# A mixture-of-experts stage: tokens become the stationary operand, expert weights are read in place

## The chip, the cores and the metric

The kernel runs on one core of one Trainium2 chip. The metric is the device time of one execution in microseconds. The times come from repeated executions; the profile is one execution recorded by the hardware profiler.

## What is computed

8192 tokens of width 256 are normalised (layer norm) to `xn`. A state-space block with a gated feed-forward works on `xn`, and so does a mixture of 32 experts with 8 chosen per token and one shared expert. The result is `x` plus both. The part that matters here, for the normalised tokens `h`:

```python
combine = (jax.nn.one_hot(tki, E, dtype=tkw.dtype) * tkw[..., None]).sum(1)
g = jax.nn.silu(jnp.einsum('th,eih->tei', h, w_gate))
u = jnp.einsum('th,eih->tei', h, w_up)
routed = jnp.einsum('tei,ehi->th', g * u * combine[:, :, None], w_down)
```

An expert has a hidden width of 128: gate and up weights are 128 x 256 each, the down weight 256 x 128. All is fp32.

## The kernel before

The program is written by hand engine by engine, with semaphores; the order of each engine's instructions is the order in the code. It has four parts. First, all tokens are normalised and routed. Then nine groups of 512 tokens go through the state-space block and feed-forward (`pe_group` and its like), while GpSimd scatters the token rows, sorted by expert, into `sorted_rows` in HBM, a row for each of the 8 choices. Then comes the expert stage. Last come the other seven groups, beside which GpSimd gathers the experts' results and VectorE sums them.

The expert stage treats 576 tiles of 128 sorted rows, each of one expert, in 288 pairs (`ALL`), 144 for each half of the tokens. All expert weights lie in SBUF in `big` (`WEXP` = 768 columns an expert: gate and up, then down). Which expert a tile has is known only at run time: `te_row` holds offsets, loaded into registers, four for two pairs. For pair n:

- SyncE loads two tiles of rows (`load_rows`, L427) into `rows[n % 4]`, a ring of 4. A row has 256 values and 32 routing weights.
- PE turns them: 4 transposes (`r_transpose`, L1255). ScalarE copies them out of PSUM to `rT` (L647).
- VectorE copies the gate/up weights of the pair's two experts from `big` to `wgu` (`copy_weights`, L1031), two pairs ahead.
- PE forms gate and up (`e_gu`, L1266), with weights stationary and tokens moving: 8 products, each 2 passes (a weight load and a matmul each) in the trace. The result has hidden units on the partitions.
- ScalarE takes the SiLU of gate (`e_gate`, L652), VectorE multiplies with up to `eh` (`e_hidden`, L1039).
- PE multiplies by the down weights (`e_down`, L1280), `eh` stationary and the weights moving in place out of `big`: 2 products of 256 columns, 4 passes.
- ScalarE and VectorE scale one tile each by the routing weight (`e_out`, L662 and L1048) to `ey`.
- SyncE stores the results (L449), and then loads the rows of pair n + 4.

PE's order in iteration n is `e_gu(n)`, `r_transpose(n+1)`, `e_down(n-1)`. ScalarE's is gate(n), `rT` copy(n+1), output(n-1). VectorE's is weight copies(n+2), hidden(n), output(n-1), and from pair 150 on a step of summing gathered results (L957, L964). SyncE's order is output store, rows load, and now and then a load of `parts` and a store of `out`. GpSimd scatters the second half's rows during the first part of the stage (until 853 us), and gathers the first half's results from 1042 us on.

Of the kernel before, what the change touches and what calls it, by code (L numbers as in the profile page):

```python
# [5 lines left out]
P = 128  # L6
# [3 lines left out]
ALU = mybir.AluOpType  # L10
# [39 lines left out]
def build(nc, x, log_lambda, BT, CT, D_skip, ssm_w, ssm_w_col, ffn_w_col, w13T, w2T, gateT, gate_bias, wexp,  # L50
# [29 lines left out]
    with ExitStack() as ctx:  # L80
# [3 lines left out]
        def sem(name):  # L84
            return ctx.enter_context(nc.semaphore(name))
# [91 lines left out]
        def take(n):  # L177
            at[0] += n
            assert at[0] <= ARENA
            return arena[:, at[0] - n:at[0]]  # L180
# [23 lines left out]
        wgu = [take(4 * INNER * 2).rearrange("p (s w) -> p s w", s=2) for _ in range(2)]  # L204
# [68 lines left out]
        wgu_ready = sem("wgu_ready")  # L273
# [58 lines left out]
        def scattered_all(eng, half):  # L332

            for j in range(4):
                eng.wait_ge(scattered[half][j], 16 * K * QUARTER)
# [3 lines left out]
        def _(sp):  # L339
# [106 lines left out]
            for n in range(ALL):  # L446
                sp.wait_ge(ey_act, n + 1)
                sp.wait_ge(ey_dve, n + 1)
                sp.dma_start(pair_rows(results, n), ey[n % RING]).then_inc(ey_stored[n % RING], 16)  # L449
                if n + RING == PAIRS:  # L450
                    scattered_all(sp, 1)
                if n + RING < ALL:
                    load_rows(n + RING)
                for i in summed_after(n + 6):
                    load_part(i)
                for i in summed_after(n - 2):
                    store_out(i)
            assert not summed_after(ALL - 2) and not summed_after(ALL - 1)

            sp.wait_ge(wgu_ready, ALL)  # L460
# [70 lines left out]
        def _(act):  # L531
# [107 lines left out]
            regs = [[act.alloc_register(f"act_expert{j}_{k}") for k in range(4)] for j in range(3)]  # L639

            def load_experts(n):
                act.load(regs[n // 2 % 3], te_row[0:1, HALVES * NTILE + 2 * n:HALVES * NTILE + 2 * n + 4])

# [12 lines left out]
            def e_out(n):  # L656

                e = act.snap(regs[n // 2 % 3][2 * (n % 2)], min_val=0, max_val=E - 1)
                act.wait_ge(ey_ready, n + 1)
                if n >= RING:  # L660
                    act.wait_ge(ey_stored[n % RING], 16 * (n // RING))
                nc.scalar.activation(ey[n % RING][:, 0, :], ps[:, 4 + 2 * (n % 2), 0:D], ACT.Copy,  # L662
                                     scale=rows[n % RING][:, 0, ds(e + D, 1)]).then_inc(ey_act, 1)
# [5 lines left out]
            for n in range(ALL):  # L669
                if n % 2 == 0:  # L670
                    load_experts(n)
                e_gate(n)
                if n + 1 < ALL:
                    rT_copy(n + 1)
                if n >= 1:
                    e_out(n - 1)
# [12 lines left out]
        def _(dve):  # L689
# [328 lines left out]
            offsets = [[dve.alloc_register(f"dve_offset{j}_{k}") for k in range(4)] for j in range(3)]  # L1018
            experts = [[dve.alloc_register(f"dve_expert{j}_{k}") for k in range(4)] for j in range(3)]

            def load_tables(n):
                dve.load(offsets[n // 2 % 3], te_row[0:1, 2 * n:2 * n + 4])
                dve.load(experts[n // 2 % 3], te_row[0:1, HALVES * NTILE + 2 * n:HALVES * NTILE + 2 * n + 4])

            def copy_weights(n):

                if n >= 2:
                    dve.wait_ge(egu_ready, n - 1)
                for s in range(2):
                    at_w = dve.snap(offsets[n // 2 % 3][2 * (n % 2) + s], min_val=0, max_val=(E - 1) * WEXP)  # L1030
                    last = nc.vector.tensor_copy(wgu[n % 2][:, s, :], big[:, ds(at_w, 4 * INNER)])  # L1031
                last.then_inc(wgu_ready, 1)

            def e_hidden(n):

                dve.wait_ge(eg_ready, n + 1)
                if n >= 2:
                    dve.wait_ge(ey_ready, n - 1)
                tt(eh[n % 2], eg[n % 2], ps[:, 2 + n % 2, :].rearrange("p (s u i) -> p s u i", s=2, u=2)[:, :, 1, :],  # L1039
                   ALU.mult).then_inc(eh_ready, 1)  # L1040

            def e_out(n):

                e = dve.snap(experts[n // 2 % 3][2 * (n % 2) + 1], min_val=0, max_val=E - 1)
                dve.wait_ge(ey_ready, n + 1)
                if n >= RING:
                    dve.wait_ge(ey_stored[n % RING], 16 * (n // RING))
                tsc(ey[n % RING][:, 1, :], ps[:, 5 + 2 * (n % 2), 0:D], rows[n % RING][:, 1, ds(e + D, 1)], None,  # L1048
                    ALU.mult).then_inc(ey_dve, 1)
# [5 lines left out]
            load_tables(0)  # L1055
            copy_weights(0)
            copy_weights(1)
            for n in range(ALL):
                if n + 2 < ALL:
                    if n % 2 == 0:  # L1060
                        load_tables(n + 2)
                    copy_weights(n + 2)
                e_hidden(n)
                if n >= 1:
                    e_out(n - 1)
                for i, j in sum_after(n):
                    sum_step(i, j)
            e_out(ALL - 1)
# [15 lines left out]
        def _(pe):  # L1084
# [173 lines left out]
            def e_gu(n):  # L1258

                pe.wait_ge(rT_ready, n + 1)  # L1260
                pe.wait_ge(wgu_ready, n + 1)
                for s in range(2):
                    for u in range(2):
                        for c in range(DC):
                            at_w = (2 * c + u) * INNER
                            last = mm(ps[:, 2 + n % 2, (2 * s + u) * P:(2 * s + u + 1) * P],  # L1266
                                      wgu[n % 2][:, s, at_w:at_w + INNER],
                                      rT[n % 2][:, (2 * s + c) * P:(2 * s + c + 1) * P],
                                      start=c == 0, stop=c == DC - 1)
                last.then_inc(egu_ready, 1)  # L1270

            def e_down(n):

                if n >= 2:
                    pe.wait_ge(ey_act, n - 1)
                    pe.wait_ge(ey_dve, n - 1)
                pe.wait_ge(eh_ready, n + 1)
                for s in range(2):
                    at_w = pe.snap(regs[n // 2 % 3][2 * (n % 2) + s], min_val=0, max_val=(E - 1) * WEXP)
                    last = mm(ps[:, 4 + 2 * (n % 2) + s, 0:D], eh[n % 2][:, s, :], big[:, ds(at_w + 2 * D, D)],  # L1280
                              start=True, stop=True)
                last.then_inc(ey_ready, 1)
# [6 lines left out]
            for n in range(ALL):  # L1289
                if n % 2 == 0:  # L1290
                    load_offsets(n)
                e_gu(n)
                if n + 1 < ALL:
                    r_transpose(n + 1)
                if n >= 1:
                    e_down(n - 1)
# [54 lines left out]
```

## Time and profile before

| | us |
|---|---|
| median of 3 runs | 1920.8 (1915.5 to 1921.8) |
| the profiled execution's own time | 1924.6 |
| its span, first to last instruction | 1922.9 |
| PE busy | 1772.2 (92%) |
| GpSimd busy | 1058.2 (55%) |
| VectorE busy | 1016.6 (53%) |
| ScalarE busy | 652.8 (34%) |
| mean granted TensorE clock | 0.968 |

PE is TensorE's matmul side and PEld its weight loads, which overlap it; DVE is VectorE, ACT ScalarE, POOL GpSimd, SP SyncE. A "q" behind an engine's name is its sequencer (register work, DMA issues). L1266 is line 1266 of the kernel. Matmul durations are modelled: starts can be trusted more than ends. The expert stage lies between 551 and 1552 us of the span.

### The profile page before, as it was taken

To read this page: it belongs to the slowest core of one execution; us is meant where nothing else is said; L and a number is where in the kernel's file an instruction comes from. 1 tells how busy PE (TensorE), PEld (TensorE's weight loads), DVE (VectorE), ACT (ScalarE), POOL (GpSimd) and SP (SyncE) were. 2 spreads that over 40 slices of the span, in tenths; PEclk is the share of its full clock that TensorE was granted. 3 is DMA by queue.
4 is the path that set the end of the run, shared out by engine and by line. 5 is a ranking of instruction groups with operands and counts; after the bars stand their busy time and mean duration, and the time that the engine had idled before them with its cause. 6 is when DMAs were issued, how large, how long until landed. Compare 5 with 4: busy or idle time off the path is not lost.

```text
span 1922.9 us, 30939 instructions
## 1 busy us (share of the span) xinstructions
PE 1772.2 (92%) x9896; PEld 1347.3 (70%) x9896; DVE 1016.6 (53%) x2464; ACT 652.8 (34%) x1349; POOL 1058.2 (55%) x1058
## 2 busy tenths in 40 slices
PE   6798898999989999999999999899989969999995
PEld 3454555666568888888988888788878846666663
DVE  6577456333334444444444656565656635565554
ACT  5621222222224444444444434343434422222220
POOL 0002777777777777750002655556555147777776
PEclk9898898999989999999999999999999979999997
DMA  6804334554668988985556888788777753333333
GB/s 208 257 22 138 136 127 162 198 213 157 237 225 276 286 272 282 284 261 175 175 171 199 255 242 250 242 243 245 237 238 241 212 168 113 114 114 101 107 103 105
DMA packets 262614, 374.53 MB, mean 195 GB/s; under 512 B 30917, under 2 KB 227641, under 8 KB 261689
## 3 DMA queue, kind: packets, MB, share of 16 engines
q1 hardware_dynamic: 212392, 227.51, 38.5%
q0 software_dynamic: 49920, 145.03, 22.9%
q8 instruction: 82, 1.34, 0.3%
q14 instruction: 76, 0.61, 0.1%
q10 hardware_dynamic: 144, 0.03, 0.0%
HBM read 189.47 MB, written 182.98 MB: 194 GB/s over the span
## 4 chain that ended last, share of the span: by engine, by line
PE 67%; DMA 17%; DVE 8%; issue 3%; SPq 2%; ACT 1%; DVEq 1%; POOL 1%; POOLq 0%; ACTq 0%
PE ps L1182 19%; DMA arena<-sorted_rows 16%; PE ps L1266 15%; PE ps L1199 11%; PE ps L1280 9%; PE ps L1255 6%; DVE arena L1048 2%; PE ps L1135 2%; PE ps L1164 1%; SPq L449 1%; PE ps L1151 1%; PE ps L1102 1%; PE ps L1174 1%; DMA big<-in_x 1%; POOL xe L524 1%
## 5 line engine op out<-in xcount | busy, mean ns | idle before, releaser
L524 POOL DMA_INDIRECT xe<-results,slots x512 | 537.4, 1050 | 524.7 <-DMA results<-arena 239.2
L1266 PE MATMUL ps<-arena 128*128 128x128 f32 x4608 | 590.5, 282 | 1.5 <-ACT arena L647 1.5
L1266 PEld LDWEIGHTS ps<-arena 128*128 128x128 f32 x4608 | 540.2, 193 | 66.0 <-ACT arena L647 65.9
L1031 DVE COPY arena<-big 128x512 f32 x576 | 226.6, 435 | 344.4 <-PE ps L1266 320.6
L513 POOL DMA_INDIRECT sorted_rows<-big,slots x256 | 257.6, 1006 | 85.0 <-issue 77.7
L1280 PE MATMUL ps<-big,arena 128*128 x1152 | 297.5, 381 | 0.3 <-DVE arena L1039 0.3
L513 POOL DMA_INDIRECT sorted_rows<-xe,slots x256 | 251.8, 983 | 78.0 <-issue 78.0
L1182 PE MATMUL ps<-arena,w 128*128 128x512 f32 x640 | 287.7, 592 | 0.0
L939 DVE TENSOR_TENSOR arena<-arena,ps 128x512 f32<-128x512 f32 (+1 forms) x128 | 88.1, 688 | 330.7 <-ACT arena L615 329.6
L615 ACT ACTIVATE arena<-ps 128x512 f32<-128x512 f32 (+1 forms) x128 | 76.3, 596 | 546.7 <-PE ps L1182 502.7
L652 ACT ACTIVATE arena<-ps 128x256 f32<-128x256 f32 x288 | 110.4, 383 | 378.8 <-PE ps L1266 378.8
L1255 PE MATMUL ps<-ident,arena 128*128 128x128 f32 x1152 | 180.7, 280 | 59.9 <-DMA arena<-sorted_rows 58.4
L1280 PEld LDWEIGHTS ps<-big,arena 128*128 128x128 f32 x1152 | 197.2, 191 | 15.4 <-issue 0.7
L647 ACT ACTIVATE arena<-ps 128x512 f32<-128x512 f32 x288 | 172.0, 597 | 102.7 <-PE ps L1255 91.9
L1182 PEld LDWEIGHTS ps<-arena,w 128*128 128x128 f32 x640 | 121.8, 190 | 118.8 <-issue 114.7
L1048 DVE TENSOR_SCALAR arena<-ps,arena 128x256 f32<-128x256 f32 x288 | 139.3, 484 | 122.2 <-PE ps L1280 120.8
L1199 PE MATMUL ps<-w,arena 128*128 128x256 f32 (+1 forms) x768 | 186.4, 386 | 1.8 <-DVE arena L939 1.8
L1255 PEld LDWEIGHTS ps<-ident,arena 128*128 128x128 f32 x1152 | 129.6, 142 | 79.4 <-DMA arena<-sorted_rows 71.3
L1199 PEld LDWEIGHTS ps<-w,arena 128*128 128x128 f32 (+1 forms) x768 | 143.1, 191 | 50.7 <-issue 31.2
L662 ACT ACTIVATE arena<-ps,arena 128x256 f32<-128x256 f32 x288 | 136.3, 473 | 109.1 <-PE ps L1280 109.1
L957 DVE TENSOR_TENSOR xe<-xe 128x1024 f32<-128x1024 f32 (+2 forms) x192 | 148.9, 775 | 9.8 <-DMA xe<-results,slots 7.2
L1182 PE MATMUL ps<-arena,shgu 128*128 128x512 f32 x256 | 123.5, 639 | 7.0 <-DVEq L793 7.0
(158 smaller groups left out, 1175.5 us busy)
## 6 DMA issues: line engine op xcount, KB each, us to landing
arena<-sorted_rows SPq DMA_DIRECT2D x288, 288.0 KB, 3.7
results<-arena SPq DMA_DIRECT2D x288, 256.0 KB, 2.8
big<-in_x SPq DMA_DIRECT2D x32, 512.0 KB, 4.3
sorted_rows<-big SPq DMA_DIRECT2D x2, 4608.0 KB, 16.9
xe<-results,slots POOLq DMA_INDIRECT x512, 3.3
out<-xe SPq DMA_DIRECT2D x64, 128.0 KB, 2.2
sorted_rows<-big SPq DMA_DIRECT2D x48, 144.0 KB, 1.8
big<-in_wexp SPq DMA_DIRECT2D x1, 5632.0 KB, 20.6
```

The lines of the kernel that those rows point to most:

```text
L513: pool.indirect_dma_start(out=sorted_rows[half], out_offset=bass.IndirectOffsetOnAxis(ap=slots[:, half * HT + t, k:k + 1], axis=0), in_=ro ...
L524: pool.indirect_dma_start(out=gathered_at[i % RING][:, k, :], out_offset=None, in_=results[half], in_offset=bass.IndirectOffsetOnAxis(ap=s ...
L647: nc.scalar.activation(rT[n % 2], ps[:, n % 2, :], ACT.Copy).then_inc(rT_ready, 1)
L662: nc.scalar.activation(ey[n % RING][:, 0, :], ps[:, 4 + 2 * (n % 2), 0:D], ACT.Copy, scale=rows[n % RING][:, 0, ds(e + D, 1)]).then_inc(ey ...
L957: do(tt(y[:, 0:m, :], y[:, 0:m, :], y[:, m:2 * m, :], ALU.add))
L1031: last = nc.vector.tensor_copy(wgu[n % 2][:, s, :], big[:, ds(at_w, 4 * INNER)])
L1048: tsc(ey[n % RING][:, 1, :], ps[:, 5 + 2 * (n % 2), 0:D], rows[n % RING][:, 1, ds(e + D, 1)], None, ALU.mult).then_inc(ey_dve, 1)
L1182: last = mm(ps[:, 2 + 2 * (s % 2) + u, :], w[:, u, c, lo:lo + P], src[:, c, :], start=c == 0, stop=c == DC - 1)
L1199: last = mm(ps[:, 6 + t // 2, (t % 2) * D:(t % 2 + 1) * D], h[c % HR][at_p, t * P:(t + 1) * P], w, start=False, stop=s == CH - 1 and t % 2 ...
L1255: last = tp(ps[:, n % 2, j * P:(j + 1) * P], rows[n % RING][:, s, c * P:(c + 1) * P], ident[:, :])
L1266: last = mm(ps[:, 2 + n % 2, (2 * s + u) * P:(2 * s + u + 1) * P], wgu[n % 2][:, s, at_w:at_w + INNER], rT[n % 2][:, (2 * s + c) * P:(2 * ...
L1280: last = mm(ps[:, 4 + 2 * (n % 2) + s, 0:D], eh[n % 2][:, s, :], big[:, ds(at_w + 2 * D, D)], start=True, stop=True)
```

## The change

The product's operands change sides. The turned tokens `rT` become the stationary operand of gate and up, and the weights move in place out of `big`, 256 columns (gate and up of one 128-row chunk) at once; VectorE's copies to `wgu` go. Now tokens lie on the partitions of the result, so the routing weight is applied in `e_hidden` as a per-partition factor, and not on the outputs. The hidden product must be turned before the down product: `h_transpose` (2 transposes) and VectorE's `ehT_copy` are new, and the down product and outputs come one iteration later. SyncE's loop issues `load_rows(m+4)` once `e_hidden(m)` is done, and the store of pair m - 2 behind it.

```diff
-        wgu = [take(4 * INNER * 2).rearrange("p (s w) -> p s w", s=2) for _ in range(2)]
+        ehT = [take(2 * P).rearrange("p (s n) -> p s n", n=P) for _ in range(2)]
...
-            for n in range(ALL):
+            for m in range(ALL + 2):
+                if m < ALL:
+                    sp.wait_ge(eh_ready, m + 1)
+                    if m + RING == PAIRS:
+                        scattered_all(sp, 1)
+                    if m + RING < ALL:
+                        load_rows(m + RING)
+                n = m - 2
+                if n < 0:
+                    continue
                 sp.wait_ge(ey_act, n + 1)
                 sp.wait_ge(ey_dve, n + 1)
                 sp.dma_start(pair_rows(results, n), ey[n % RING]).then_inc(ey_stored[n % RING], 16)
-                if n + RING == PAIRS:
-                    scattered_all(sp, 1)
-                if n + RING < ALL:
-                    load_rows(n + RING)
...
-            sp.wait_ge(wgu_ready, ALL)
...
-                nc.scalar.activation(ey[n % RING][:, 0, :], ps[:, 4 + 2 * (n % 2), 0:D], ACT.Copy,
-                                     scale=rows[n % RING][:, 0, ds(e + D, 1)]).then_inc(ey_act, 1)
+                nc.scalar.activation(ey[n % RING][:, 0, :], ps[:, 4 + 2 * (n % 2), 0:D], ACT.Copy
+                                     ).then_inc(ey_act, 1)
...
-                if n >= 1:
-                    e_out(n - 1)
+                if n >= 2:
+                    e_out(n - 2)
+            e_out(ALL - 2)
             e_out(ALL - 1)
...
             def e_hidden(n):
 
                 dve.wait_ge(eg_ready, n + 1)
                 if n >= 2:
+                    dve.wait_ge(hposed, n - 1)
+                for s in range(2):
+                    e = dve.snap(experts[n // 2 % 2][2 * (n % 2) + s], min_val=0, max_val=E - 1)
+                    last = nc.vector.scalar_tensor_tensor(eh[n % 2][:, s, :], eg[n % 2][:, s, :],
+                                                          rows[n % RING][:, s, ds(e + D, 1)],
+                                                          ps[:, 2 + n % 2, (2 * s + 1) * P:(2 * s + 2) * P],
+                                                          ALU.mult, ALU.mult)
+                last.then_inc(eh_ready, 1)
+
+            def ehT_copy(n):
+                dve.wait_ge(hposed, n + 1)
+                if n >= 2:
                     dve.wait_ge(ey_ready, n - 1)
-                tt(eh[n % 2], eg[n % 2], ps[:, 2 + n % 2, :].rearrange("p (s u i) -> p s u i", s=2, u=2)[:, :, 1, :],
-                   ALU.mult).then_inc(eh_ready, 1)
+                nc.vector.tensor_copy(ehT[n % 2], ps[:, 4 + 2 * (n % 2), D:2 * D].rearrange("p (s n) -> p s n", n=P)
+                                      ).then_inc(ehT_ready, 1)
...
-            load_tables(0)
-            copy_weights(0)
-            copy_weights(1)
             for n in range(ALL):
-                if n + 2 < ALL:
-                    if n % 2 == 0:
-                        load_tables(n + 2)
-                    copy_weights(n + 2)
+                if n % 2 == 0:
+                    load_experts(n)
                 e_hidden(n)
                 if n >= 1:
-                    e_out(n - 1)
+                    ehT_copy(n - 1)
+                if n >= 2:
+                    e_out(n - 2)
                 for i, j in sum_after(n):
                     sum_step(i, j)
...
                 pe.wait_ge(rT_ready, n + 1)
-                pe.wait_ge(wgu_ready, n + 1)
                 for s in range(2):
-                    for u in range(2):
-                        for c in range(DC):
-                            at_w = (2 * c + u) * INNER
-                            last = mm(ps[:, 2 + n % 2, (2 * s + u) * P:(2 * s + u + 1) * P],
-                                      wgu[n % 2][:, s, at_w:at_w + INNER],
-                                      rT[n % 2][:, (2 * s + c) * P:(2 * s + c + 1) * P],
-                                      start=c == 0, stop=c == DC - 1)
+                    at_w = pe.snap(regs[n // 2 % 3][2 * (n % 2) + s], min_val=0, max_val=(E - 1) * WEXP)
+                    for c in range(DC):
+                        last = mm(ps[:, 2 + n % 2, s * D:(s + 1) * D], rT[n % 2][:, (2 * s + c) * P:(2 * s + c + 1) * P],
+                                  big[:, ds(at_w + 2 * c * INNER, 2 * INNER)], start=c == 0, stop=c == DC - 1)
                 last.then_inc(egu_ready, 1)
 
-            def e_down(n):
-
+            def h_transpose(n):
                 if n >= 2:
                     pe.wait_ge(ey_act, n - 1)
                     pe.wait_ge(ey_dve, n - 1)
                 pe.wait_ge(eh_ready, n + 1)
                 for s in range(2):
+                    last = tp(ps[:, 4 + 2 * (n % 2), D + s * P:D + (s + 1) * P], eh[n % 2][:, s, :], ident[:, :])
+                last.then_inc(hposed, 1)
+
+            def e_down(n):
+                pe.wait_ge(ehT_ready, n + 1)
+                for s in range(2):
                     at_w = pe.snap(regs[n // 2 % 3][2 * (n % 2) + s], min_val=0, max_val=(E - 1) * WEXP)
-                    last = mm(ps[:, 4 + 2 * (n % 2) + s, 0:D], eh[n % 2][:, s, :], big[:, ds(at_w + 2 * D, D)],
+                    last = mm(ps[:, 4 + 2 * (n % 2) + s, 0:D], ehT[n % 2][:, s, :], big[:, ds(at_w + 2 * D, D)],
                               start=True, stop=True)
                 last.then_inc(ey_ready, 1)
...
                 if n >= 1:
-                    e_down(n - 1)
+                    h_transpose(n - 1)
+                if n >= 2:
+                    e_down(n - 2)
+            h_transpose(ALL - 1)
+            e_down(ALL - 2)
             e_down(ALL - 1)
```

## Rows read from the trace of the kernel before

**Rows 1.** The page, part 1: busy time and share of each engine.

```profile
PE 1772.2 (92%) x9896; PEld 1347.3 (70%) x9896; DVE 1016.6 (53%) x2464; ACT 652.8 (34%) x1349; POOL 1058.2 (55%) x1058
```

**Rows 2.** The page, part 4: the chain that ended last, by line.

```profile
PE ps L1182 19%; DMA arena<-sorted_rows 16%; PE ps L1266 15%; PE ps L1199 11%; PE ps L1280 9%; PE ps L1255 6%; DVE arena L1048 2%; PE ps L1135 2%; PE ps L1164 1%; SPq L449 1%; PE ps L1151 1%; PE ps L1102 1%; PE ps L1174 1%; DMA big<-in_x 1%; POOL xe L524 1%
```

**Rows 3.** Three stretches: length, busy PE, PEld, DVE, ACT, POOL, granted clock, DMA share, GB/s.

```profile
560.00:853.00 293.00, 280.76 (x2075) 251.79 (x2075) 139.17 (x345) 125.17 (x259) 223.82 (x228) 1.00 0.89 278
853.00:1040.00 187.00, 184.22 (x1389) 167.79 (x1388) 91.60 (x232) 84.18 (x174) 0.92 (x1) 1.00 0.59 175
1040.00:1550.00 510.00, 471.06 (x3416) 418.34 (x3415) 300.59 (x695) 206.82 (x427) 270.97 (x256) 0.99 0.79 239
```

**Rows 4.** Timeline, one pair at 903 us: start, duration, what, idle before it.

```profile
902.78 1.86 PEld L1266 LDWEIGHTS ps<-arena 128*128 128x128 f32 x16 [0.22 <-ACT arena L647]
...
903.09 0.47 ACT L662 ACTIVATE arena<-ps,arena 128x256 f32<-128x256 f32 x1 [0.37 <-PE ps L1280]
903.11 0.48 DVE L1048 TENSOR_SCALAR arena<-ps,arena 128x256 f32<-128x256 f32 x1 [0.22 <-PE ps L1280]
...
904.08 0.47 SPq L427 DMA_DIRECT2D arena<-sorted_rows  x1
...
904.66 0.60 PE L1255 MATMUL ps<-ident,arena 128*128 128x128 f32 x4
904.87 0.38 ACT L652 ACTIVATE arena<-ps 128x256 f32<-128x256 f32 x1 [1.30 <-PE ps L1266]
904.97 0.76 DVE L1031 COPY arena<-big 128x512 f32 x2 [1.38 <-PE ps L1266]
...
905.10 1.03 PE L1280 MATMUL ps<-big,arena 128*128 x4
905.30 0.60 ACT L647 ACTIVATE arena<-ps 128x512 f32<-128x512 f32 x1
905.65 0.41 DVE L1039 TENSOR_TENSOR arena<-arena,ps 128x256 f32<-128x256 f32 x1
905.95 1.86 PEld L1266 LDWEIGHTS ps<-arena 128*128 128x128 f32 x16 [0.22 <-ACT arena L647]
```

**Rows 5.** Line 1266: duration ns min/median/max, first and last start.

```profile
L1266 PEld LDWEIGHTS ps<-arena x4608: 186/192/338, 553.5 to 1548.8; 128*128 128x128 f32 x192
```

**Rows 6.** Waits of weight loads, 553 to 1552 us: total us, times, longest.

```profile
PEld ps L1255 <- DMA arena<-sorted_rows: 71.3, 92, 2.7
PEld ps L1266 <- ACT arena L647: 65.9, 287, 1.2
```

**Rows 7.** Row loads (L427): 880 to 960, then 1200 to 1350, then all.

```profile
DMA to landing us min/median/max: 2.9/3.0/4.4
...
L427 SPq DMA_DIRECT2D arena<-sorted_rows x42: 463/472/1057, 1199.6 to 1349.2; - x42
...
  PEld ps L1255: 19.7, 20
DMA to landing us min/median/max: 2.8/4.4/5.5
...
DMA to landing us min/median/max: 2.8/3.7/6.3
```

**Rows 8.** Timeline, the last pair of the stage.

```profile
1549.61 0.42 DVE L1039 TENSOR_TENSOR arena<-arena,ps 128x256 f32<-128x256 f32 x1 [1.68 <-ACT arena L652]
...
1550.28 0.73 PEld L1280 LDWEIGHTS ps<-big,arena 128*128 128x128 f32 x4 [0.66 <-issue]
```

**Rows 9.** Line 1247, the load of offsets on PE's sequencer: duration ns.

```profile
L1247 PEldq TENSOR_LOAD <-te_row x144: 328/522/894, 551.7 to 1542.4; - x144
```

**Rows 10.** Timeline, the first pair of the stage.

```profile
553.51 3.49 PEld L1266 LDWEIGHTS ps<-arena 128*128 128x128 f32 x16 [1.17 <-ACT arena L647]
```

**Rows 11.** A three-operand instruction (L908), and the longest summing step, 560 to 1552.

```profile
L908 DVE SCALAR_TENSOR_TENSOR arena<-big,rinv,skip_w x60: 459/479/544, 85.4 to 1841.8; 128x256 f32<-128x256 f32 x60
L957 DVE TENSOR_TENSOR xe<-xe 128x1024 f32<-128x1024 f32 x32 | 38.9, 1216 | 0.0
```

More of the change, by code:

```diff
@@ L272, in build @@
         rT_ready = sem("rT_ready")
-        wgu_ready = sem("wgu_ready")
+        hposed = sem("hposed")
+        ehT_ready = sem("ehT_ready")
         egu_ready = sem("egu_ready")
@@ L636, in _ @@
                 act_group(g, g + 1 < FIRST)
-            regs = [[act.alloc_register(f"act_expert{j}_{k}") for k in range(4)] for j in range(3)]
-            def load_experts(n):
-                act.load(regs[n // 2 % 3], te_row[0:1, HALVES * NTILE + 2 * n:HALVES * NTILE + 2 * n + 4])
             def rT_copy(n):
@@ L656, in e_out @@
             def e_out(n):
-                e = act.snap(regs[n // 2 % 3][2 * (n % 2)], min_val=0, max_val=E - 1)
                 act.wait_ge(ey_ready, n + 1)
@@ L669, in _ @@
             for n in range(ALL):
-                if n % 2 == 0:
-                    load_experts(n)
                 e_gate(n)
@@ L1015, in _, with load_experts @@
                 dve_group(g, g + 1 < FIRST)
[L1018 to L1032, printed above, removed]
+            experts = [[dve.alloc_register(f"dve_expert{j}_{k}") for k in range(4)] for j in range(2)]
+            def load_experts(n):
+                dve.load(experts[n // 2 % 2], te_row[0:1, HALVES * NTILE + 2 * n:HALVES * NTILE + 2 * n + 4])
             def e_hidden(n):
@@ L1037, in e_hidden @@
                 if n >= 2:
+                    dve.wait_ge(hposed, n - 1)
[9 more added lines that the diff above has]
+                if n >= 2:
                     dve.wait_ge(ey_ready, n - 1)
-                tt(eh[n % 2], eg[n % 2], ps[:, 2 + n % 2, :].rearrange("p (s u i) -> p s u i", s=2, u=2)[:, :, 1, :],
-                   ALU.mult).then_inc(eh_ready, 1)
+                nc.vector.tensor_copy(ehT[n % 2], ps[:, 4 + 2 * (n % 2), D:2 * D].rearrange("p (s n) -> p s n", n=P)
+                                      ).then_inc(ehT_ready, 1)
             def e_out(n):
-                e = dve.snap(experts[n // 2 % 3][2 * (n % 2) + 1], min_val=0, max_val=E - 1)
                 dve.wait_ge(ey_ready, n + 1)
@@ L1047, in e_out @@
                     dve.wait_ge(ey_stored[n % RING], 16 * (n // RING))
-                tsc(ey[n % RING][:, 1, :], ps[:, 5 + 2 * (n % 2), 0:D], rows[n % RING][:, 1, ds(e + D, 1)], None,
-                    ALU.mult).then_inc(ey_dve, 1)
+                nc.vector.tensor_copy(ey[n % RING][:, 1, :], ps[:, 5 + 2 * (n % 2), 0:D]).then_inc(ey_dve, 1)
             dve.wait_ge(te_loaded, 16 * 2 * HALVES)
@@ L1054, in _ @@
                 dve.wait_ge(part_stored[par], 16 * len(range(par, FIRST, 2)))
-            load_tables(0)
-            copy_weights(0)
-            copy_weights(1)
             for n in range(ALL):
-                if n + 2 < ALL:
-                    if n % 2 == 0:
-                        load_tables(n + 2)
-                    copy_weights(n + 2)
+                if n % 2 == 0:
+                    load_experts(n)
                 e_hidden(n)
                 if n >= 1:
-                    e_out(n - 1)
+                    ehT_copy(n - 1)
+                if n >= 2:
+                    e_out(n - 2)
                 for i, j in sum_after(n):
                     sum_step(i, j)
+            ehT_copy(ALL - 1)
+            e_out(ALL - 2)
             e_out(ALL - 1)
```

## The prediction

> **What bounds the kernel now.** Read the page from the top. TensorE (PE) is busy 92% of the span and no other engine above 55% [rows 1], but that is a share over the whole program, and the change touches one stage, the 288 expert pairs. The chain that ended last gives 16% of the span, about 307 us, to the load of a pair's rows [rows 2]. That figure must not be taken for idle time: the chain follows one ring of dependences (load, transpose, products, output, next load) and books the whole flight of each load, while PE works on other pairs under most of it. So I went to PE itself.
>
> Three stretches of the stage [rows 3], at 24 PE instructions a pair: 2075 instructions are 86.5 pairs in 293 us, 3.39 us a pair, while the second half is still scattered; 57.9 pairs in 187 us, 3.23 us, when GpSimd is nearly silent; 142.3 pairs in 510 us, 3.58 us, while results are gathered. The same work takes different times, and the stretch with the least foreign DMA traffic is the fastest.
>
> One pair of the quiet stretch [rows 4] shows the floor. The first weight load of `e_gu` starts at 902.78 and, one pair on, at 905.95: 3.17 us. Inside, 16 gate/up passes are (1.86 - 0.19)/15 = 0.111 us apart, 1.78 us; the 4 row transposes (0.60 - 0.27)/3 = 0.110 apart, 0.44; the 4 down passes (1.03 - 0.38)/3 = 0.217 apart, 0.87. That is 3.09. The missing 0.08 to 0.09 stands in the last row: the loads sat idle 0.22 us until ScalarE's copy `rT` (905.30 + 0.60 = 905.90) was done; the load wants to start some 0.1 before its matmul, and came 0.09 late.
>
> Over the stage, the first gate/up load starts at 553.5 and the last at 1548.8 [rows 5]; less 15 x 0.111, that is 993.6 us for 287 periods, where 287 x 3.18 = 912.7 would do. The excess is 81 us. The waits name it: the transpose's weight load waited 71.3 us in 92 places for the rows' DMA [rows 6] (each wait is counted from the end of a 0.19 us load, where the next could have started at 0.11, so 92 x 0.08 = 7 us more are hidden in it: 79). The other wait, 65.9 us in 287 places for the copy `rT`, is the 0.09 a pair above.
>
> Why are rows late? SyncE issues `load_rows(n+4)` after the output of pair n. In [rows 4] it goes out at 904.08 and its transpose comes at 904.66 + 3.17 = 907.83: 3.75 us of slack. Landing takes 3.0 us (median) in the quiet stretch, but 4.4 (up to 5.5) while gathers run, with 20 waits in 42 [rows 7]. The load is launched too late for its latency under load.
>
> **The change, part by part.**
>
> *PE, gate and up.* Eight products (16 passes of 128 columns) become four of 256 columns, 8 passes. Same shape and operands as the down product, which moves `big` over 256 columns at 0.217 a pass: 8 x 0.217 = 1.74 against 1.78, -0.04.
>
> *PE, hidden transposes.* Two more, same form as the row transposes: 2 x 0.110 = +0.22. Their wait (hidden of pair n-1) was satisfied most of a period before. The down product is now that of n-2 and waits for a copy also made in the period before.
>
> *PE, the copy's cover.* Between the row transposes and the next `e_gu` now lie 0.22 + 0.87 us in place of 0.87. Counted from the last row transpose (x = 904.66 + 0.33 = 904.99), `rT` is done at x + 0.91, and the first gate/up load would be due at x + 0.11 + 0.22 + 0.87 - 0.11 = x + 1.09. The wait now sits on a register operation (the offset into `big`), which before ran far ahead. From the end of a releaser to a plain load is 0.05 us (905.90 to 905.95) [rows 4]; over a register operation on ScalarE 0.13 (906.13 to 903.09 + 3.17 = 906.26) [rows 4]; on PE over two sequencer steps, at the stage's end, 0.25 (VectorE ends 1550.03, load at 1550.28) [rows 8]. The load thus starts at x + 0.96, 1.04 or 1.16: nothing, nothing, or 0.07 late. I take nothing, nearest to the single step: the old 0.09 goes. The table load (0.52, at most 0.89 us [rows 9]) now feeds the same iteration; it is queued before the wait, and there is room for it while PE is in the 1.5 us of transposes and down products.
>
> Sum of a period: 8 x 0.217 + 6 x 0.110 + 4 x 0.217 = 3.26 us against 3.17 to 3.18. **PE's own work becomes longer**, by 0.08 x 287 = 23 us over the stage.
>
> *SyncE, the order of loads.* `load_rows(m+4)` now waits for the hidden product of pair m, since the routing weight is applied there, and not for the outputs. With e_gu(m) starting at G: its last pass ends at G + 1.51 + 0.38 = G + 1.9, the gate takes 0.38 and starts 0.04 later, the two hidden instructions about 0.6, so the issue is near G + 3.1. The transpose comes at G + 3 x 3.26 + 1.74 = G + 11.5. Slack 8.4 us, against 3.75, and the longest landing of the whole stage is 6.3 [rows 7]. The store of a pair is issued one iteration later and a part load or output store may stand before a load; each holds the queue for about the 0.47 us of an issue [rows 4], covered by the slack. Behind the new wait stands the store of pair m-2, whose outputs come later still (near G + 3.9), so it loses nothing. The wait on the weight copies ahead of the late `x` loads goes as well, worth nothing: it was long satisfied. So the row waits go: -81 + 3 that I leave for stray ones and 2 for the first pair, which ran at half clock (its 16 loads took 3.49 us [rows 10]) and stays so. That is about -76.
>
> *VectorE.* Gone: two copies of 512 columns, 0.76 together, and the scaled output (0.48). In: two hidden products of 128 columns in place of one of 256 (0.41), a copy `ehT`, a plain output copy. Bounds for the two: 0.41 (same columns at once) to 2 x 0.48 (a three-operand instruction of twice the width [rows 11]); the copies 0.41 to 0.48 each. VectorE's pair is 1.2 to 1.9 us against 1.65, plus summing of at most 1.22 [rows 11] in a pair: under 3.26 either way. It costs the sum nothing; were its cover gone it would be the 0.2 us by which 3.1 nears 3.26. ScalarE only loses a register step.
>
> *Gathers.* GpSimd starts them when half 0 is stored, one iteration later: some 7 us after e_gu(145) starts, the eighth lands near +20, and the first sum is due near 5 x 3.26 + 3.9 = +20. A wait of 1 or 2 us, once, hidden by the hidden product's lead.
>
> *Tail.* After the last `e_gu`, a transpose (0.22, and 0.27 until its end), a copy (0.42), and the register step now stand before the last down product, and the hidden product is two instructions: +1.2 us. The late groups behind are unchanged and follow it one for one.
>
> **The sum.** New stage: 287 x 3.26 + 2 + 3 = 940.6; old 993.6; difference -53.0, with the tail -51.8. From the profiled execution's own time, 1924.6 (span 1922.9): 1873. The median of the runs is 3.8 lower: 1869, rounded **1870**. Its own range: no stray waits and a period of 3.25 give 1863; 10 us of stray waits and 0.03 a pair more, 1885.
>
> - *The row waits are throughput, not latency*, **slower than before** (8%). The 16 DMA engines are busy 0.89 and 0.79 in the stretches with waits, 0.59 without [rows 3]. If loads queue behind each other, launching them early only lengthens their landing; the point of decision is a landing over 8.4 us. Then the 81 us stay, and PE's extra 23 us hide under them or come on top: with the tail +1 to +24, so 1922 to 1945, and 1940 as its value, since most pairs have no wait to hide under. Against it: rows and results alone need 0.59 x 3.23 = 1.9 us of the engines a pair, so in the scatter stretch 0.89 - 1.9/3.39 = 0.33 is foreign, and 1.9/3.26 + 0.33 = 0.91 at the new pace: still below 1.
> - *VectorE turns into the wait* (4%): a gather that is late holds the queue of sums, hidden products and the new copy together. 0.1 us a pair in the 144 pairs with sums, and some row waits: 1885 to 1915.
> - *The clock falls* with the larger share of transposes (1%). The first pair, run at the lower level, shows the price: passes (3.49 - 0.23)/15 = 0.217 apart where later ones are 0.111 [rows 10], twice the time. A tenth of the stage's work at 1.2 GHz adds 94 us, 1964.
> - *The change does not do what it says*, that is passes over `big` at register addresses pace worse than 0.217 (2%): with 0.02 each, 8 x 0.02 x 287 = 46 us, 1916.
>
> **How the numbers follow.** Forecast 70%, the rivals 30%. 1853 to 1900 holds the forecast, what lies a little below it, and the exposed register step: 85% by these chances; the slower rivals stay outside. Within 0.3% (about 6 us, what a measurement of this kernel can tell) lie the last rival, the mild end of the throughput one and of the VectorE one, 4%. Slower are most of the throughput rival and the clock, 8%; faster 88%.
>
> **What would show it.** In the profile after: `e_gu`'s period 3.26 in the quiet stretch, with 8 passes 0.217 apart and no idle before them; almost no wait of the row transpose for DMA; SyncE's load issued about 8 us before its transpose; the stage from 553.5 to some 1500. A period of 3.3 or more with PE idle until ScalarE's copy is the first rival; landings of 8 us are the second. The prediction is wrong if either stands.

## The result: 1864 us, and where it came from

| kernel | median us | ratio to before, 95% interval |
|---|---|---|
| before | 1920.2 (1915.5 to 1921.8) | |
| changed | 1864.2 (1863.9 to 1868.5) | 0.9708 [0.9672, 0.9743] |

The change makes the kernel 3% faster; 1870 with a range of 1853 to 1900 was predicted. The profiled execution took 1864.3 us, with a span of 1862.4.

The page of the changed kernel, its busy times (part 1) and its chain by line (part 4), answering to [rows 1, 2]:

```profile
PE 1764.0 (95%) x8166; PEld 1323.1 (71%) x8168; DVE 949.2 (51%) x2464; ACT 627.5 (34%) x1349; POOL 1033.7 (56%) x1058
PE ps L1260 27%; PE ps L1178 19%; PE ps L1277 13%; PE ps L1195 11%; PE ps L1251 7%; PE ps L1270 3%; PE ps L1160 2%; PE ps L1131 2%; PE ps L1098 1%; PE ps L1147 1%; PE ps L1170 1%; DMA big<-in_x 1%; POOL xe L529 1%; PE ps L1091 1%; SPq L366 0%
```

In the new numbering L1251 is the row transposes, L1260 gate and up, L1270 the hidden transposes, L1277 the down products, L428 the row load. The row load had 16% of the chain [rows 2] and is gone from it. PE's busy time hardly moved (1772 to 1764 us); what went is the time between its instructions. The stage's stretches, read as [rows 3]:

```profile
560.00:853.00 293.00, 293.00 (x1626) 257.25 (x1625) 122.72 (x360) 122.91 (x270) 218.22 (x227) 1.00 0.89 287
853.00:1040.00 187.00, 187.00 (x1039) 164.17 (x1038) 78.30 (x231) 78.83 (x173) 6.70 (x7) 1.00 0.57 177
1040.00:1490.00 450.00, 449.14 (x2489) 394.00 (x2488) 264.68 (x683) 188.26 (x414) 244.43 (x249) 1.00 0.87 262
```

At 18 PE instructions a pair that is 3.24, 3.24 and 3.25 us a pair, where it was 3.39, 3.23 and 3.58. The quiet stretch became a little slower, the other two faster: foreign DMA traffic no longer shows in PE's pace. One pair on the timeline (start, duration, what), answering to [rows 4]:

```profile
903.51 0.37 SPq L428 DMA_DIRECT2D arena<-sorted_rows  x1
903.51 1.64 PEld L1260 LDWEIGHTS ps<-big,arena 128*128 128x128 f32 x8
903.66 1.89 PE L1260 MATMUL ps<-big,arena 128*128 x8
...
905.17 0.58 PEld L1251 LDWEIGHTS ps<-ident,arena 128*128 128x128 f32 x4
905.39 0.60 PE L1251 MATMUL ps<-ident,arena 128*128 128x128 f32 x4
905.59 0.38 ACT L652 ACTIVATE arena<-ps 128x256 f32<-128x256 f32 x1 [1.34 <-PE ps L1260]
...
905.83 0.38 PE L1270 MATMUL ps<-ident,arena 128*128 128x128 f32 x2
906.03 0.60 ACT L647 ACTIVATE arena<-ps 128x512 f32<-128x512 f32 x1
906.04 1.03 PE L1277 MATMUL ps<-big,arena 128*128 x4
906.13 0.60 DVE L1028 SCALAR_TENSOR_TENSOR arena<-arena,ps 128x128 f32<-128x128 f32 x2 [1.84 <-ACT arena L652]
906.65 0.41 DVE L1038 COPY arena<-ps 128x256 f32<-128x256 f32 x1
906.76 0.37 SPq L428 DMA_DIRECT2D arena<-sorted_rows  x1
906.76 0.78 PEld L1260 LDWEIGHTS ps<-big,arena 128*128 128x128 f32 x4
```

The period is 906.76 - 903.51 = 3.25 us, and no weight load of PE shows an idle time ahead of it. `rT` is done at 906.03 + 0.60 = 906.63, and the first gate/up load starts 0.13 later. A row load goes out at 906.76, 0.03 after the hidden products of the pair four before it (906.13 + 0.60).

The first and last gate/up loads (line view, in ns), and who waited for the row loads with their landing, answering to [rows 5 to 7]:

```profile
L1260 PEld LDWEIGHTS ps<-big,arena x2304: 186/190/337, 550.9 to 1486.3; 128*128 128x128 f32 x192
...
  PE ps L1251: 6.0, 1
DMA to landing us min/median/max: 2.7/3.9/6.5
```

From 550.9 to 1486.3, less 7 x 0.216 for the last group, is 933.9 us for 287 periods, 3.25 each and 2 us more for the first; it was 993.6. The 6.0 us is one wait before the stage begins. So the 71.3 us in 92 waits [rows 6] are all gone, though landings are no shorter than before (3.9 and 6.5 against 3.7 and 6.3 [rows 7]).

The account of the 60.5 us between the spans: 59.7 in the 287 periods, 2.6 because the stage's first product starts earlier (550.9 for 553.5; in the profiles of all the kernels here it lies between 550.9 and 554.6 and follows none of the edits, so this part is chance), and 1.8 given back behind the last `e_gu` (before: 1922.9 - 1547.1 = 375.8 us from its first load to the end, now 1862.4 - 1484.8 = 377.6).

### The profile page after: what moved, and what is told of

Read it like the earlier page. It is cut to its first block, busy times and chain, and to the rows that moved or that the text cites. A ratio compares the mean times of both kernels' runs of the same rounds, so it can differ in the third digit from the quotient of the medians.

```text
span 1862.4 us, 27141 instructions
## 1 busy us (share of the span) xinstructions
PE 1764.0 (95%) x8166; PEld 1323.1 (71%) x8168; DVE 949.2 (51%) x2464; ACT 627.5 (34%) x1349; POOL 1033.7 (56%) x1058
## 4 chain that ended last, share of the span: by engine, by line
PE 89%; DVE 6%; DMA 1%; issue 1%; ACT 1%; POOL 1%; SPq 1%; POOLq 0%; DVEq 0%; ACTq 0%
PE ps L1260 27%; PE ps L1178 19%; PE ps L1277 13%; PE ps L1195 11%; PE ps L1251 7%; PE ps L1270 3%; PE ps L1160 2%; PE ps L1131 2%; PE ps L1098 1%; PE ps L1147 1%; PE ps L1170 1%; DMA big<-in_x 1%; POOL xe L529 1%; PE ps L1091 1%; SPq L366 0%
## 5 line engine op out<-in xcount | busy, mean ns | idle before, releaser
L529 POOL DMA_INDIRECT xe<-results,slots x512 | 517.5, 1011 | 490.8 <-DMA results<-arena 232.8
L1260 PE MATMUL ps<-big,arena 128*128 x2304 | 546.4, 380 | 2.2 <-ACT arena L647 2.2
L1260 PEld LDWEIGHTS ps<-big,arena 128*128 128x128 f32 x2304 | 427.9, 190 | 73.5 <-issue 3.0
L1028 DVE SCALAR_TENSOR_TENSOR arena<-arena,ps 128x128 f32<-128x128 f32 x576 | 175.0, 344 | 467.3 <-ACT arena L652 393.6
L1277 PE MATMUL ps<-big,arena 128*128 x1152 | 296.2, 380 | 0.0
L518 POOL DMA_INDIRECT sorted_rows<-xe,slots x256 | 246.3, 962 | 78.1 <-issue 78.1
L652 ACT ACTIVATE arena<-ps 128x256 f32<-128x256 f32 x288 | 110.7, 384 | 390.9 <-PE ps L1260 390.9
L1277 PEld LDWEIGHTS ps<-big,arena 128*128 128x128 f32 x1152 | 196.4, 190 | 14.9
L1251 PE MATMUL ps<-ident,arena 128*128 128x128 f32 x1152 | 173.6, 273 | 6.0 <-DMA arena<-sorted_rows 6.0
L1251 PEld LDWEIGHTS ps<-ident,arena 128*128 128x128 f32 x1152 | 144.8, 142 | 35.5 <-issue 6.6
L661 ACT ACTIVATE arena<-ps 128x256 f32<-128x256 f32 x288 | 110.6, 384 | 141.7 <-PE ps L1277 141.7
L955 DVE TENSOR_TENSOR xe<-xe 128x1024 f32<-128x1024 f32 (+2 forms) x192 | 149.0, 776 | 10.3 <-DMA xe<-results,slots 7.7
L1046 DVE COPY arena<-ps 128x256 f32<-128x256 f32 x288 | 122.0, 424 | 10.7 <-PE ps L1277 0.9
```

What stands on the lines that cost most here:

```text
L518: pool.indirect_dma_start(out=sorted_rows[half], out_offset=bass.IndirectOffsetOnAxis(ap=slots[:, half * HT + t, k:k + 1], axis=0), in_=ro ...
L529: pool.indirect_dma_start(out=gathered_at[i % RING][:, k, :], out_offset=None, in_=results[half], in_offset=bass.IndirectOffsetOnAxis(ap=s ...
L652: nc.scalar.activation(eg[n % 2], ps[:, 2 + n % 2, :].rearrange("p (s u i) -> p s u i", s=2, u=2)[:, :, 0, :], ACT.Silu).then_inc(eg_ready, 1)
L955: do(tt(y[:, 0:m, :], y[:, 0:m, :], y[:, m:2 * m, :], ALU.add))
L1028: last = nc.vector.scalar_tensor_tensor(eh[n % 2][:, s, :], eg[n % 2][:, s, :], rows[n % RING][:, s, ds(e + D, 1)], ps[:, 2 + n % 2, (2 * ...
L1046: nc.vector.tensor_copy(ey[n % RING][:, 1, :], ps[:, 5 + 2 * (n % 2), 0:D]).then_inc(ey_dve, 1)
```

## The experiments

The theory: the gain is the earlier row load; turning the products round costs PE 0.07 us a pair. Rival A: the waits were throughput of the DMA engines. Rival B: the gain is in the products or in VectorE's relief. All ratios are against the kernel before, run on the same chip.

### The old kernel with five row tiles

```diff
     RING = 4
+    RR = 5
...
+        rows.append(take(2 * ROW).rearrange("p (s w) -> p s w", w=ROW))
...
+            load_rows(RING)
...
-                if n + RING < ALL:
-                    load_rows(n + RING)
+                if n + RR < ALL:
+                    load_rows(n + RR)
```

> The kernel before with one change: the ring of row tiles has five places in place of four, so that a pair's rows are loaded one pair (3.2 us) earlier. Products, VectorE's weight copies and the routing weight on the outputs stay as before. Theory (the time comes from the row loads' latency, and the turned products only cost): slack 3.75 + 3.18 = 6.9 us against landings of at most about 6.5, so the 81 us of excess go but for some 5, the period stays 3.18: 1842 to 1850, that is faster than the changed kernel by about 15 to 20. Rival A (throughput of the DMA engines): landings grow by 3 us, time stays near 1920. Rival B (the gain comes from the products or from VectorE's relief): 1920 too.

Measured: 1844.4 us, ratio 0.9605 [0.9579, 0.9631]. The row loads' landing (line view), the scatter and gather stretches (columns as in [rows 3]), and one period on PE's timeline:

```profile
DMA to landing us min/median/max: 2.8/4.1/6.9
```

```profile
560.00:853.00 293.00, 292.85 (x2214) 267.39 (x2213) 148.52 (x369) 134.16 (x277) 219.86 (x226) 1.00 0.93 291
...
1040.00:1460.00 420.00, 420.00 (x3177) 383.77 (x3177) 284.42 (x657) 192.31 (x397) 242.42 (x239) 1.00 0.88 272
```

```profile
899.89 1.86 PEld L1269 LDWEIGHTS ps<-arena 128*128 128x128 f32 x16 [0.22 <-ACT arena L650]
...
903.07 1.86 PEld L1269 LDWEIGHTS ps<-arena 128*128 128x128 f32 x16 [0.22 <-ACT arena L650]
```

The period is still 3.18 with its wait for `rT`, and now everywhere: the load alone gives more than the whole change. Landings did not grow by the 3 us that A asks for, with the DMA engines busier than before (0.93 and 0.88): the median went from 3.7 to 4.1, the longest from 6.3 to 6.9. B is out as the source of the gain, for no product was touched. The turned products cost 1864.2 - 1844.4 = 20 us, where (3.25 - 3.18) x 287 = 20; from its first to its last gate/up load the stage takes 913.9 us here and 933.9 in the changed kernel.

### The changed kernel with later loads

```diff
-                    sp.wait_ge(eh_ready, m + 1)
+                    sp.wait_ge(eh_ready, min(m + 2, ALL))
```

> The changed kernel with each row load waiting for the hidden product of one pair later: slack 8.4 - 3.25 = 5.1 us. Theory: median landing 3.9, a few land later than 5.1: 1864 to 1874. Rival A (throughput): the start of a load makes no difference, 1864.

And later still:

```diff
-                    sp.wait_ge(eh_ready, m + 1)
+                    sp.wait_ge(egu_ready, min(m + 3, ALL))
```

> The changed kernel with each row load waiting for the gate/up product of two pairs later: slack 3.25 + 1.73 - 1.9 = 3.1 us, somewhat under the 3.75 of the kernel before. Theory: a ring of two pairs, 2 x period = 3.5 + landing; 3.25 a pair at a landing of 3.0 (quiet stretch), 3.8 at 4.1 (230 busy pairs), so about +100 to +130 us, 1960 to 1995, with PE waiting for the rows' DMA. Rival A (throughput): 1864. Rival B (the turned products are the gain): 1864 or little more.

Measured: 1882.8 us, 0.9799 [0.9772, 0.9826], for the first, and 1976.3, 1.029 [1.0253, 1.0328], for the second. Who waited for the row loads (us, times), first and second:

```profile
  PEld ps L1251: 14.1, 21
DMA to landing us min/median/max: 2.8/3.9/6.5
```

```profile
  PEld ps L1251: 142.2, 217
DMA to landing us min/median/max: 2.7/3.5/6.8
```

The second run hit its range, and it is slower than the kernel before: without the early load, this form of the products loses. The start of the load decides, and not its traffic. The first run missed by 9 us. A timeline at the first summing step shows a part of it:

```profile
1056.15 1.22 DVE L955 TENSOR_TENSOR xe<-xe 128x1024 f32<-128x1024 f32 x1 [5.80 <-DMA xe<-results,slots]
...
1058.16 0.37 SPq L428 DMA_DIRECT2D arena<-sorted_rows  x1
...
1058.87 0.20 PEld L1270 LDWEIGHTS ps<-ident,arena 128*128 128x128 f32 x2 [3.32 <-issue]
```

VectorE waited 5.8 us for the first gather, with the next hidden product behind it; PE and the next row load waited in turn. In SyncE's queue the store of results stood behind the load's longer wait. It goes out 0.47 us after the next pair's first gate/up load (903.73 and 903.26), where the changed kernel's goes 0.85 after its own (904.36 and 903.51): 3.25 + 0.47 - 0.85 = 2.9 us later.

### The same with the store ahead of the load's wait

```diff
             for m in range(ALL + 2):
+                n = m - 2
+                if n >= 0:
+                    sp.wait_ge(ey_act, n + 1)
+                    sp.wait_ge(ey_dve, n + 1)
+                    sp.dma_start(pair_rows(results, n), ey[n % RING]).then_inc(ey_stored[n % RING], 16)
                 if m < ALL:
-                    sp.wait_ge(eh_ready, m + 1)
+                    sp.wait_ge(eh_ready, min(m + 2, ALL))
...
-                n = m - 2
                 if n < 0:
                     continue
-                sp.wait_ge(ey_act, n + 1)
-                sp.wait_ge(ey_dve, n + 1)
-                sp.dma_start(pair_rows(results, n), ey[n % RING]).then_inc(ey_stored[n % RING], 16)
```

> The run with loads one pair later (1883 where 1864 to 1874 was expected), now with SyncE storing pair m-2 before it waits for the load of m+4. There the store stood behind the load's wait and left 2.6 us late; the first gather landed late, VectorE waited 5.8 us for it, and PE 5.5 us in two pairs. Theory: that 5.5 goes and the 20 single waits on late landings stay: 1876 to 1879. Rival (all 19 us are late landings): 1883.

Measured: 1872.1 us, 0.9721 [0.9691, 0.9752]. The waits of PE's weight loads in the stage:

```profile
PEld ps L1252 <- DMA arena<-sorted_rows: 7.3, 13, 1.3
```

The late store cost 10.7 us by the medians (15 by the ratios; the stage itself is 10.3 shorter), twice or more what I gave it: besides the stall at the first sum, the waits on landings fell, from 14.1 us in 21 to 7.3 in 13. Why the order of the store spares landings stays open. In the changed kernel a load goes out at 903.51 and its transposes come two periods after those at 905.17, at 911.67: 8.16 us. One pair less, 4.91, leaves only these few waits, so most of that slack is reserve.

### The changed kernel with VectorE's copies put back

```diff
+        unused = [take(4 * INNER) for _ in range(4)]
...
+                for s in range(2):
+                    nc.vector.tensor_copy(unused[2 * (n % 2) + s], big[:, ((2 * n + s) % E) * WEXP:((2 * n + s) % E) * WEXP + 4 * INNER])
                 e_hidden(n)
```

> The changed kernel with VectorE's two copies of 512 weight columns a pair put back (into a tile that nobody reads). Theory: VectorE has 0.8 us to spare in every pair even with a summing step, so 1864, within 2 us. Rival B (VectorE's relief is part of the gain): the copies take up to 0.76 us a pair back, up to +200 us if nothing covers them, some +10 to +60 if only the pairs with sums suffer.

Measured: 1865.3 us, 0.9723 [0.9693, 0.9754]. The busy line of its page:

```profile
PE 1764.4 (95%) x8168; PEld 1323.2 (71%) x8168; DVE 1159.7 (62%) x3040; ACT 627.6 (34%) x1349; POOL 1054.7 (57%) x1058
```

VectorE does 210 us more and the kernel is 1 us longer, within the spread of its runs (1864.8 to 1871.5): its relief was worth nothing that can be measured.

### The changed kernel with the hidden transposes first

```diff
                 e_gu(n)
+                if n >= 1:
+                    h_transpose(n - 1)
                 if n + 1 < ALL:
                     r_transpose(n + 1)
-                if n >= 1:
-                    h_transpose(n - 1)
```

> The changed kernel with PE's two hidden transposes ahead of the row transposes, so that they no longer cover the copy rT. PE's work is the same. Theory (the loop row transposes, rT, register step, gate/up takes 3.20 us without them and lies just under the 3.25 of PE's work): period 3.20 + 0.22 = 3.42, 287 x 0.17 = +48, 1912. Rival (only PE's work counts): 1864.

Measured: 1914.8 us, 0.9955 [0.9932, 0.9978]. Timeline:

```profile
901.52 0.60 PE L1251 MATMUL ps<-ident,arena 128*128 128x128 f32 x4
...
902.15 0.60 ACT L647 ACTIVATE arena<-ps 128x512 f32<-128x512 f32 x1 [0.27 <-PE ps L1251]
...
902.89 1.38 PEld L1260 LDWEIGHTS ps<-big,arena 128*128 128x128 f32 x7 [0.31 <-issue]
```

The same instructions in another order cost 51 us (47 by the ratios), nearly all of the gain. `rT` ends at 902.75, and the load starts 0.14 later, after 0.31 without a load; the next pair's starts at 906.31, so the period is 3.42, as forecast. The profile books the wait as "issue", probably because it sits on a register operation of the sequencer. The loop's length could be read in the changed kernel itself. Its second period has no down product in it yet, so that only the loop is left, and takes 559.32 - 556.12 = 3.20 us:

```profile
556.12 1.59 PEld L1260 LDWEIGHTS ps<-big,arena 128*128 128x128 f32 x8 [1.01 <-issue]
...
559.32 1.59 PEld L1260 LDWEIGHTS ps<-big,arena 128*128 128x128 f32 x8 [0.79 <-issue]
```

### The old kernel with the row transposes inside gate and up

```diff
                 for s in range(2):
+                    if s == 1 and n + 1 < ALL:
+                        r_transpose(n + 1)
                     for u in range(2):
...
                 e_gu(n)
-                if n + 1 < ALL:
-                    r_transpose(n + 1)
...
-                e_gate(n)
                 if n + 1 < ALL:
                     rT_copy(n + 1)
+                e_gate(n)
```

With five row tiles (the first experiment's edit as well):

> The kernel before with five row tiles, and the next pair's row transposes put in the middle of the gate/up products (ScalarE copies rT before the gate). The copy rT then has 0.89 + 0.87 us of PE work as cover in place of 0.87. Theory: the 0.09 us a pair that PE waits for rT goes, period 16 x 0.111 + 0.44 + 0.87 = 3.09, stage 287 x 3.09 + 2 = 889: 1817 to 1828, the upper end if the slack of the rows (6.9 - 0.9 = 6.0) lets some landings show. Rival (the 0.22 us of idle loads at that place is no real loss, the period is set by the passes alone): 1844, as with five row tiles alone.

With four, as before:

> The kernel before with its four row tiles and the row transposes in the middle of gate/up: PE's wait for rT goes, but rows are needed 0.9 us earlier, slack 2.8 us in place of 3.75. Theory: the ring of four pairs closes at (9.5 + landing)/4, 3.13 us a pair when landing is 3.0, and 3.5 to 3.65 in the 230 busy pairs: 1912 to 1948, no gain or a loss. Rival A (throughput of the DMA engines): the row waits do not change, 0.09 x 287 = 26 us less, 1895.

Measured: 1825.3 us, 0.9485 [0.945, 0.9521], with five; 2028.7, 1.0535 [1.0492, 1.0577], with four. With five, the old wait for `rT` is gone (its gate/up loads show no idle before them), and the period lost its 0.09 as priced:

```profile
901.01 1.08 PEld L1271 LDWEIGHTS ps<-arena 128*128 128x128 f32 x8
...
904.10 0.52 PEld L1271 LDWEIGHTS ps<-arena 128*128 128x128 f32 x3
```

That is 3.09 us. With four, the theory had the direction and missed the size by 80 us. In the quiet stretch:

```profile
995.81 1.03 PE L1282 MATMUL ps<-big,arena 128*128 x4
...
997.12 0.48 DVE L1048 TENSOR_SCALAR arena<-ps,arena 128x256 f32<-128x256 f32 x1
...
998.08 0.47 SPq L427 DMA_DIRECT2D arena<-sorted_rows  x1
...
1001.07 0.42 PEld L1255 LDWEIGHTS ps<-ident,arena 128*128 128x128 f32 x4 [0.24 <-DMA arena<-sorted_rows]
...
1002.45 1.03 PE L1282 MATMUL ps<-big,arena 128*128 x4
```

and over the stage (waits of PE's weight loads):

```profile
PEld ps L1255 <- DMA arena<-sorted_rows: 188.5, 197, 3.4
```

Follow the ring: from a down product (995.81) to the load 2.27 us, to landing 2.99, and from there to a down product (1002.45) 1.38. The load is that of the pair four on, but this down product is that of the pair two on: in PE's order the transposes of pair n + 4 stand ahead of the down product of pair n + 2, so whatever holds them holds it too, and with it the load of pair n + 6. So 2 x period = 3.65 + landing: 3.32 in the quiet stretch and 3.7 to 3.9 at the medians of 3.7 and 4.1 under traffic, against the (9.5 + landing)/4 that I had written. The measured mean over the stage is 3.8; by stretches, at 24 instructions a pair:

```profile
560.00:853.00 293.00, 250.20 (x1851) 231.72 (x1850) 119.22 (x310) 112.24 (x232) 223.22 (x228) 1.00 0.83 262
930.00:1050.00 120.00, 113.62 (x839) 104.80 (x838) 51.65 (x139) 50.55 (x104) 0.00 (x0) 1.00 0.54 162
1100.00:1600.00 500.00, 411.05 (x2949) 380.42 (x2948) 258.09 (x610) 178.78 (x369) 256.53 (x243) 0.97 0.72 217
```

That is 3.80, 3.43 and 4.07, 0.1 to 0.2 above the ring at median landings. A part of it in the last stretch is the clock, which I had not priced: PE stood idle 2.9 us until 1175.79, for rows that had been asked for at 1170.16, and from about 1175 to 1182 the granted clock was 0.50, the level of 1.2 GHz. A mean of 0.97 over 500 us is an estimated 15 us of PE's work lost in this way.

### Load and store swapped in SyncE's queue

```diff
-                sp.dma_start(pair_rows(results, n), ey[n % RING]).then_inc(ey_stored[n % RING], 16)
                 if n + RING == PAIRS:
                     scattered_all(sp, 1)
                 if n + RING < ALL:
                     load_rows(n + RING)
+                sp.dma_start(pair_rows(results, n), ey[n % RING]).then_inc(ey_stored[n % RING], 16)
```

> The kernel before with one change in SyncE's order: once the outputs of pair n are done, it issues the row load of n+4 first and the store of n behind it (the load went out 0.41 us later before). Slack 3.75 + 0.41 = 4.16 us. Theory, with the ring closed over two pairs as the last run asks (2 x period = 2.6 + landing before, 2.2 + landing now): up to 0.2 us a pair less in the pairs that wait, 86 at about 0.15 and 142 at about 0.2, so about -40 of the 81 us: 1880, 1870 to 1895. Rival (throughput): no change.

> The fastest kernel so far (five row tiles, row transposes in the middle, 1825) with the same swap of load and store. Its load goes out 5.5 us before the transpose, now 5.9; 10 us of stray waits are left in it. Theory: half of them go, 1820, 1816 to 1824. The store is 0.4 us later, which may cost a gather wait in VectorE once, up to 3 us.

Measured: 1880.0 us, 0.9778 [0.9735, 0.9822], for the old kernel with nothing but the swap; 1820.7, 0.947 [0.9429, 0.9511], for the fastest one. Both fell in their ranges, the first where the corrected ring put it. PE's waits for row loads, old kernel with the swap and fastest kernel:

```profile
PEld ps L1255 <- DMA arena<-sorted_rows: 31.0, 49, 2.0
```

```profile
PEld ps L1258 <- DMA arena<-sorted_rows: 1.5, 4, 0.7
```

From 71.3 us in 92 waits [rows 6] to 31.0 in 49, by issuing one DMA 0.41 us earlier. For the fastest kernel the swap's 4.6 us lie within the two intervals, but the stage, from its first to its last gate/up load, went from 897.7 to 890.5 us, as its waits did (8.2 to 1.5). The last version is 2.3% faster than the changed kernel (1820.7 to 1864.2; 2.5% by the ratios) and keeps the old operands.

## Why the prediction was right

- **What bounds.** Right. The 81 us of excess over 287 equal periods were rows that landed late; five tiles in the old kernel removed them and nothing else. A little of the 81 was the clock, which the prediction did not look for there: behind two waits of over 2 us the granted clock was 0.50 for about 3.4 us each (from 1127.8 and 1424.8), an estimated 3.4 us of work in all. In the changed kernel it stays at 1.00.
- **Gate and up, hidden transposes.** 3.26 us a period forecast, 3.25 measured. The passes over `big` at run-time addresses pace like the down product's: from 903.66, eight take 1.89, (1.89 - 0.38)/7 = 0.216. The rival that they do not falls.
- **The copy's cover and the register step.** The single step, 0.13, was the right one of the three: `rT` to load is 0.13 in the changed kernel. PE loses nothing, but by little: the loop without its cover is 3.20 and PE's work 3.25. The rival of an exposed step was 0.05 us a pair away, and the hidden transposes, which I had counted as a cost of 0.22, are also what keeps it away.
- **SyncE's order.** Slack of 8.4 forecast, 8.16 measured; the runs with later loads give the waits back as it shrinks.
- **The number.** The sum gave 1924.6 - 51.8 = 1872.8 for the profiled execution, which took 1864.3: 8.5 us less. The 3 us left for stray waits did not come, the period was 3.247 for 3.26 (3.7 us), the stage started 2.6 earlier by chance, and the tail took back 0.6 (1.8 for 1.2). That 1870 was only 6 too high is in part luck: 3.8 us were taken off because the profiled execution of the kernel before lay above its median, and the changed kernel's does not.
- **Throughput, the slower rival.** The engines are busy 0.89 and 0.87 in the changed kernel and 0.93 in the scatter stretch of the old one with five tiles, and its landings stay under 7. The point at which it would have decided, 8.4 us, was not reached. A slower kernel was near in another way that I had not priced: with the same products and a load 5 us later it is 3% slower than before.
- **VectorE.** Its two hidden products took 0.60 together, between the bounds of 0.41 and 0.96, and its relief is worth nothing, as costed. The gather for the first sum was close, as worked out: 5.8 us of wait when the store was 2.9 us later, and in the changed kernel (its waits):

```profile
DVE xe L955 <- DMA xe<-results,slots: 0.5, 1, 0.5
```

- **The clock.** The granted clock is 1.00 in all three stretches, the level of 2.4 GHz, with 6 transposes among 18 instructions. If transposes do not count as busy (the Trainium skill, "TensorE: Matmul & The Clock Gate", Part 4: PE-mode transpose), a fifth of PE's time in them (0.65 of 3.25 us) did not show it here; the trace gives the rule no support and no refutation.

## What to carry to other kernels

Before valuing an edit by the work that it moves between engines, divide the stage's time by its periods and look at what the slowest ones wait for: here a transfer launched 3.75 us before its use, against landings of 2.8 to 6.3 us. One more place in the ring is then worth more than the arithmetic, and the cheapest fixes (one more tile, the load ahead of the store in the issuing queue) may beat the rewrite. When two short waits lie on one loop, such as ScalarE's copy between two PE stages, put independent PE work there, and close a ring of waits along each engine's own order: what stands behind a wait in its queue waits too, so that four row tiles here gave a ring of two pairs.

## What was not expected of the hardware

- Loads of 288 KB land hardly later when issued earlier (median 3.7 before), even with the 16 DMA engines busy 0.93 of a 293 us stretch: median 4.1 us, longest 6.9.
- A 0.41 us later issue of one DMA a pair costs 40 us over 288 pairs, since the wait repeats around the ring.
- The split with four tiles: 188.5 us of waits in 197 places grew out of moving the transposes 0.9 us forward, and the kernel lost 5.4%. A late transpose in the middle of a product stops everything behind it, the second half of gate and up, the gate and the down product.
- Waits for rows cost twice: behind an idle time of PE of 2.1 to 2.9 us the granted clock was 0.50 for 3.4 us in the kernel before and for nearly 7 in the split one with four row tiles.
